# Reordering the expert stage of a pre-norm attention and mixture-of-experts block: the next expert's rows and weights prepared under this one's products, the down product by halves of its contraction, and its last 64-row chunk as two column halves

## The chip, the cores and the metric

The kernel runs on one core of one Trainium2 chip. The metric is the device time of one launch in microseconds; the median of three launches is given, and beside it one execution under the hardware profiler.

## What is computed

The reference is one transformer layer over 16 sequences of 512 tokens, 512 features wide. The first half is layer norm, attention with 16 heads of 32, an output projection and a residual sum. The second half is layer norm, a router, 32 routed experts and one shared expert, and a residual sum. What the change touches is the part for the routed experts:

```python
C = int(math.ceil(CF * T / E))                 # 8192 tokens, 32 experts: 320 slots for each expert
...
Xp = x[slots_token].reshape(E, C, d)           # gather of rows, d = 512
G = jnp.einsum('ecd,edi->eci', Xp, W_gate)     # 512 -> 256
U = jnp.einsum('ecd,edi->eci', Xp, W_up)       # 512 -> 256
Y = jnp.einsum('eci,eid->ecd', jax.nn.silu(G) * U, W_down)   # 256 -> 512
Yf = Y.reshape(EC, d) * slots_w[:, None]
out = jnp.zeros((T, d), x.dtype).at[slots_token].add(Yf)
```

## The kernel before, in words

`transformer_block` runs three parts one after the other: `setup`, `sequences` (attention, router and shared expert for 16 sequences, with 8192 by 4 scatters of routing records into a table in DRAM), and `experts`. Only `experts` is changed. It has one program for each engine, tied together by semaphores; nothing is planned at run time, and the order on each engine is the order written.

Every matrix product is made of three float16 products (`product`, L194 to L198): each operand is scaled and split into a high and a low half, and high by high, high by low and low by high are summed in PSUM. The splitting of an operand takes two instructions: ScalarE writes the high half (`ACT.Copy` with a scale), and VectorE writes what is left (`scalar_tensor_tensor`: input times scale minus high half).

The 320 rows of an expert are taken as three chunks (`CS` = 3) of 128, 128 and 64 rows (`LASTC` = 64). `q` is the parity of the expert, for buffers that exist twice: the raw weights, the split weights, the gathered rows `xg`, the result `y`. For expert e:

* SyncE loads the three raw weights of expert e + 2 (`load`, L1142) as soon as VectorE has split those of expert e.
* GpSimd, in this order: indirect gathers of the rows of expert e + 2 into `xg` (`gather`, L1162, three DMAs), a copy of the slots' indices (L1180), a wait for the three finished chunks of `y` of expert e and for the scatters of expert e - 1, and three indirect DMAs that add `y` to the output in DRAM (L1190).
* TensorE: 48 matmuls for gate and up (L1226; two blocks `j` of 128 hidden features, each gate, then up, each 4 parts of the contraction times 3 float16 products, 320 columns); then the transposes of the first two chunks of rows of expert e + 1 (L1213, float32, 4 for a chunk); then the down product chunk by chunk (L1241; for each chunk, both halves `j` of the contraction, 3 matmuls of 512 columns each), with the transposes of the third chunk ahead of the third chunk's down product. The third chunk's matmuls have 64 weight columns (shape 128*64).
* ScalarE: tanh of the two gate blocks (L1272), the high halves of the hidden activations (L1275), the high halves of two chunks of transposed rows (L1262), the scaled results of the down product (L1286), and last, for expert e + 2, the high halves of the three weights (L1255).
* VectorE: the gating multiplications (L1328, L1331) of both blocks, the low halves of the hidden activations (L1334), the low halves of the transposed rows (L1316), and last the low halves of the three weights of expert e + 2 (L1308).

The transposed and split rows `xT` exist once, so the splitting of expert e + 1's rows follows the last gate and up product of expert e. The transposes go in turn to two PSUM banks (`dense2` and `o_ps`), the down results in turn to two others.

## Time and profile before

| what | us |
|---|---|
| median of 3 launches (2461.67 to 2462.29) | 2461.91 |
| the profiled execution | 2484.26 |
| its span | 2482.3 |
| setup and sequences, in the span | to about 2055 |
| experts, in the span | about 2055 to 2482 |

The profiled execution is 22.35 us longer than the median launch, and 1.96 us of it lie outside its span. Times below are positions in that span. Busy time of an engine is the union of its instructions. A matmul's duration counts from its issue to its modelled end, so successive matmuls overlap: what sets the pace is the distance from one start to the next.

### The profile page before, as it was taken

Reading aid. Unit: us, or ns where it says so; the run is one execution under the profiler, and the core shown is the slowest. Engines: PE = TensorE matmul, PEld = TensorE weight load, DVE = VectorE, ACT = ScalarE, POOL = GpSimd, SP = SyncE. Lnnn points to the kernel's source line nnn. Section 1 sums busy time; section 2 is a strip of 40 time slices with the busy share of each in tenths; the row PEclk is TensorE's granted clock in tenths of the full one; section 3 lists DMA queues with packets and bytes.
Section 4 is the critical chain, followed back from the end, with each engine's and each line's share of the span. In section 5 each row is a group of like instructions: output and inputs, shape, how many; then the busy total and the mean of one; then the engine's idle time right before and its main releaser. Section 6 shows DMA issues by size and latency. Waiting matters only on the chain. (4 is left out here: it accounts for less than half of the span.)

```text
span 2482.3 us, 48737 instructions
## 1 busy us (share of the span) xinstructions
PE 2293.4 (92%) x15466; PEld 1152.8 (46%) x15466; DVE 1584.5 (64%) x4870; ACT 1079.3 (43%) x1849; POOL 1125.8 (45%) x1622
## 2 busy tenths in 40 slices
PE   3789999999999999999999999999997786999997
PEld 1334444444444444444444444444443334666664
DVE  4355667666767676767676766666757554666664
ACT  3344444444443434444444444444432214666664
POOL 2234143444444444444344444445333534777775
PEclk8889999999999999999999999999999997999999
DMA  4212222222222222222222212121212017888886
GB/s 168 69 45 64 56 71 62 65 62 64 70 62 68 65 61 61 62 61 61 61 62 61 78 44 78 44 77 48 73 31 74 27 40 201 238 234 236 235 234 116
DMA packets 180850, 222.52 MB, mean 90 GB/s; under 512 B 37776, under 2 KB 119792, under 8 KB 180624
## 3 DMA queue, kind: packets, MB, share of 16 engines
q1 hardware_dynamic: 154000, 177.58, 24.3%
q0 software_dynamic: 26624, 42.12, 7.6%
q8 instruction: 118, 1.93, 0.4%
q14 instruction: 108, 0.88, 0.1%
HBM read 112.65 MB, written 56.46 MB: 68 GB/s over the span
## 5 line engine op out<-in xcount | busy, mean ns | idle before, releaser
L942 DVE CUSTOM_DVE_ANT_0 junk<-scores,maskrow 128x512 f16<-128x512 f32 (+3 forms) x1024 | 465.0, 486 | 186.0 <-PE scores L548 123.3
L674 ACT ACTIVATE probs<-scores_T 128x512 f32<-128x512 f32 x640 | 371.8, 597 | 206.4 <-PE scores_T L563 196.8
L1062 POOL TENSOR_SCALAR_AFFINE_SELECT probs<-probs 128x256 f32<-128x256 f32 x512 | 192.2, 414 | 305.2 <-ACT probs L674 303.9
L1071 POOL DMA_INDIRECT slots_dram<-rec,idx x256 | 257.4, 1006 | 119.1 <-issue 76.9
L548 PE MATMUL scores<-stack_k,stack_q 96*128 96x512 f16 (+3 forms) x1024 | 249.6, 305 | 57.9 <-DVE nmax L942 56.4
L563 PE MATMUL scores_T<-stack_q,stack_k 97*128 97x512 f16 (+3 forms) x1024 | 246.6, 302 | 21.3 <-ACT probs L674 9.8
L1048 POOL TENSOR_TENSOR xres<-xres,bo 128x512 f32<-128x512 f32 x64 | 81.2, 1271 | 265.3 <-DMA xres<-in_x 265.3
L196 PE MATMUL dense<-xT_hi,wqkv_hi 128*128 128x512 f16 x512 | 196.8, 384 | 1.5 <-DVE xT_lo L913 1.5
L197 PE MATMUL dense<-xT_lo,wqkv_hi 128*128 128x512 f16 x512 | 195.5, 382 | 0.0
L198 PE MATMUL dense<-xT_hi,wqkv_lo 128*128 128x512 f16 x512 | 195.5, 382 | 0.0
L1190 POOL DMA_INDIRECT out<-ex_y,ex_sidx x96 | 151.6, 1579 | 76.5 <-issue 41.0
L548 PEld LDWEIGHTS scores<-stack_k,stack_q 96*128 96x128 f16 x1024 | 96.1, 99 | 191.2 <-DVE nmax L942 102.6
L631 ACT ACTIVATE glu<-dense,bqk 128x512 f32<-128x512 f32 x128 | 88.0, 687 | 214.1 <-PE dense L198 207.4
L1054 POOL TENSOR_TENSOR split_q<-glu,split_q 128x512 f16<-128x512 f32 x64 | 74.3, 1161 | 215.0 <-ACT split_q L631 214.9
L563 PEld LDWEIGHTS scores_T<-stack_q,stack_k 97*128 97x128 f16 x1024 | 98.2, 98 | 137.9 <-ACT probs L674 15.7
L572 PE MATMUL o_ps<-probs,v 128*32 128x512 f32 (+3 forms) x2048 | 153.2, 440 | 7.8 <-POOL probs L1062 6.6
L572 PE MATMUL scores_T<-probs,ones 128*32 128x256 f32 (+3 forms) x2048 | 155.4, 436 | 3.6 <-issue 3.1
L913 DVE SCALAR_TENSOR_TENSOR xT_lo<-dense,xT_hi 128x512 f16<-128x512 f32 x128 | 86.7, 689 | 94.6 <-ACT xT_hi L622 85.7
L1168 POOL DMA_INDIRECT ex_xg<-x2n_dram,ex_gidx x96 | 120.2, 1252 | 47.1 <-POOL ex_gidx L1163 27.6
L956 DVE STREAM_TRANSPOSE denT<-scores_T 128x512 f32<-128x512 f32 x64 | 45.7, 714 | 143.7 <-PE scores_T L572 135.8
L1030 POOL TENSOR_SCALAR mv<-mv 128x1 f32<-128x1 f32 x128 | 35.6, 278 | 215.6 <-DVE mv L723 209.5
L646 ACT ACTIVATE glu<-dense 128x512 f32<-128x512 f32 x64 | 38.2, 597 | 209.9 <-PE dense L198 133.4
(229 smaller groups left out, 5520.0 us busy)
## 6 DMA issues: line engine op xcount, KB each, us to landing
stack_q<-split_q SPq DMA_DIRECT2D x384, 64.0 KB
stack_k<-split_k SPq DMA_DIRECT2D x384, 64.0 KB
out<-xres SPq DMA_DIRECT2D x67, 256.0 KB, 3.0
xres<-in_x SPq DMA_DIRECT2D x64, 256.0 KB, 2.8
x2n_dram<-x2n SPq DMA_DIRECT2D x16, 1024.0 KB, 4.3
ex_raw_wg<-in_W_gate SPq DMA_DIRECT2D x32, 512.0 KB
ex_raw_wu<-in_W_up SPq DMA_DIRECT2D x32, 512.0 KB
ex_raw_wd<-in_W_down SPq DMA_DIRECT2D x32, 512.0 KB
```

Of the source, the lines that this page charges most:

```text
L196: pe.matmul(out, w[0], x[0], start=start, stop=False)
L197: pe.matmul(out, w[0], x[1], start=False, stop=False)
L198: return pe.matmul(out, w[1], x[0], start=False, stop=stop)
L548: last = pe.matmul(bank[:, at:at + cols], c["stack_q"][0:SROWS, hg, h, qt * P:(qt + 1) * P], c["stack_k"][0:SROWS, hg, h, 0:cols], start=T ...
L563: last = pe.matmul(bank[:, at:at + cols], c["stack_k"][0:SROWS + 1, hg, h, kt * P:(kt + 1) * P], c["stack_q"][0:SROWS + 1, hg, h, kt * P:k ...
L572: last = pe.matmul(bank[h * HD:(h + 1) * HD, kt * P:SEQ], loaded(kt, h), c["probs"][:, h, PCOL[kt]:PCOL[kt] + n], start=kt == 0, stop=kt = ...
L674: act.activation(to, at, ACT.Exp, scale=SCALE / (QS * QS)).then_inc(exp_done, 1)
L942: last = dve.tensor_tensor_reduce(out=c["junk"][:, f % 2, at:at + cols], in0=ps["scores"][f % 2][:, at:at + cols], in1=c["maskrow"][:, SEQ ...
L1062: last = pool.affine_select(out=blk, in_=blk, compare_op=ALU.is_ge, fill=0.0, base=0, pattern=[[0, 2], [1, P]], channel_multiplier=-1)
L1071: pool.indirect_dma_start(out=a["slots"], out_offset=bass.IndirectOffsetOnAxis(ap=c["idx"][:, t, k:k + 1], axis=0), in_=c["rec"][:, t, k, ...
L1168: pool.indirect_dma_start(out=e_["xg"][q][0:r, ch, :], out_offset=None, in_=a["x2n"], in_offset=bass.IndirectOffsetOnAxis(ap=e_["gidx"][q] ...
L1190: pool.indirect_dma_start(out=a["out"], out_offset=bass.IndirectOffsetOnAxis(ap=e_["sidx"][q][0:r, ch:ch + 1], axis=0), in_=e_["y"][q][0:r ...
```

## The change

In words:

* `xT` exists twice, by parity, and the three chunks of transposes have three banks (`dense2`, `scores1`, `scores0`); the three chunks of down results have three others (`dense0`, `dense1`, `o_ps`).
* TensorE makes the transposes of the next expert's first chunk between the two blocks `j` of gate and up, and those of the second and third chunk after the second block. The down product of the two 128-row chunks is done for the first half `j` of the contraction and then for the second, with a wait for the hidden activations ahead of each half. The 64-row chunk then takes 12 matmuls of 256 columns in place of 6 of 512: the left half of the columns goes to PSUM partitions 0 to 63 and the right half to partitions 64 to 127.
* ScalarE and VectorE split the weights of expert e + 1 (not e + 2) during expert e: gate ahead of the first tanh, up after it, down later. On VectorE the low half of the down weights is the last item of the expert. The hidden activations of the first block are split before the second block is gated.
* The result of the 64-row chunk is evicted as 128 partitions by 256, and scattered as 128 half rows of 1 KB in place of 64 rows of 2 KB. For that a second table of indices (`at`) and of weights is made once, ahead of the first expert.
* SyncE's program is unchanged; the semaphore that it waits for (`w_ready`) now moves at another time.

The core of the diff:

```diff
+        out_halves = a["out"].rearrange("t (h d) -> (t h) d", h=2)
...
-            pool.wait_ge(table_ready, 2)
+            pool.wait_ge(table_ready, 1)
...
             gather(1, 1)
+            pool.wait_ge(table_ready, 5)
...
-                pool.tensor_copy(e_["sidx"][q][:, :], e_["tok"][:, bass.ds(e * CS, CS)]).then_inc(sidx_ready, 1)
+                pool.tensor_copy(e_["sidx"][q][:, :], e_["at"][:, bass.ds(e * CS, CS)]).then_inc(sidx_ready, 1)
...
                 for ch in range(CS):
-                    r = rows(ch)
+                    to, of = (a["out"], e_["y"][q][:, ch, :]) if ch < CS - 1 else (out_halves, e_["y"][q][:, ch, 0:D // 2])
...
+            T_BANK = (ps["dense"][2], ps["scores"][1], ps["scores"][0])
+            Y_BANK = (ps["dense"][0], ps["dense"][1], ps["o"])
...
             def expert(e, q, more):
-                pe.wait_ge(w_ready, (e + 1) * 3)
                 pe.wait_ge(xT_copied, (e + 1) * CS)
...
                 for j in range(JB):
                     for n, w in enumerate(("wg", "wu")):
+                        if j == 0:
+                            pe.wait_ge(w_ready, e * 3 + n + 1)
                         for k in range(DK):
...
-
+                    if j == 0 and more:
+                        transposes(e + 1, 1 - q, 0)
                 if more:
-                    transposes(e + 1, 1 - q, range(CS - 1))
-                for ch in range(CS):
-                    if ch == CS - 1 and more:
-                        transposes(e + 1, 1 - q, [ch])
...
+
+                    pe.wait_ge(glu_ready, e * 2 * JB + 2)
+                    transposes(e + 1, 1 - q, 1)
+                    transposes(e + 1, 1 - q, 2)
+                pe.wait_ge(w_ready, (e + 1) * 3)
+                for j in range(JB):
+                    pe.wait_ge(h_ready, e * JB + j + 1)
+                    for ch in range(CS - 1):
+                        if j == 0 and not is_first(e, 1):
+                            pe.wait_ge(y_ready, (e - 1) * CS + ch + 1)
+                        last = product(pe, Y_BANK[ch][:, :], both(e_["hT"], ALL, j, slice(ch * P, (ch + 1) * P)), both(e_["wd"][q], ALL, j, ALL),
+                                       j == 0, j == JB - 1)
+                        if j == JB - 1:
+                            last.then_inc(y_done, 1)
+                if not is_first(e, 1):
+                    pe.wait_ge(y_ready, e * CS)
+                for j in range(JB):
+                    h, w = both(e_["hT"], ALL, j, slice((CS - 1) * P, CAP)), both(e_["wd"][q], ALL, j, ALL)
+                    for n, (hh, ww) in enumerate(((h[0], w[0]), (h[0], w[1]), (h[1], w[0]))):
+                        for half in range(2):
+                            last = pe.matmul(Y_BANK[CS - 1][half * LASTC:(half + 1) * LASTC, 0:D // 2], hh, ww[:, half * (D // 2):(half + 1) * (D // 2)],
+                                             start=j == 0 and n == 0, stop=j == JB - 1 and n == 2)
+                last.then_inc(y_done, 1)
...
             def expert(e, q, more):
-                for j in range(JB):
...
                 if more:
-                    copies(e + 1, 1 - q, range(CS - 1))
+                    weights_hi(e + 1, 1 - q, 0)
+                tanh(e, 0)
+                if more:
+                    weights_hi(e + 1, 1 - q, 1)
+                    copies(e + 1, 1 - q, 0)
+                hidden(e, 0)
+                tanh(e, 1)
+                if more:
+                    weights_hi(e + 1, 1 - q, 2)
+                hidden(e, 1)
+                if more:
+                    copies(e + 1, 1 - q, 1)
+                    copies(e + 1, 1 - q, 2)
                 if not is_first(e, 2):
                     act.wait_ge(y_added, (e - 1) * CS * 16)
                 act.wait_ge(wcol_ready, e + 1)
                 for ch in range(CS):
...
+                    act.wait_ge(y_done, e * CS + ch + 1)
+                    cols = D if rows(ch) == P else D // 2
+                    act.activation(e_["y"][q][:, ch, 0:cols], Y_BANK[ch][:, 0:cols], ACT.Copy, scale=e_["wcol"][q][:, ch:ch + 1]).then_inc(y_ready, 1)
...
+            dve.tensor_scalar(e_["twice"][:, 0, 0:LASTC], pairs_v[:, 0:LASTC, 0], 2.0, None, ALU.mult).then_inc(table_split, 1)
+            dve.tensor_scalar(e_["twice"][:, 0, LASTC:P], pairs_v[:, 0:LASTC, 0], 2.0, 1.0, ALU.mult, ALU.add).then_inc(table_split, 1)
+            dve.tensor_copy(e_["twice"][:, 1, 0:LASTC], pairs_v[:, 0:LASTC, 1]).then_inc(table_split, 1)
+            dve.tensor_copy(e_["twice"][:, 1, LASTC:P], pairs_v[:, 0:LASTC, 1]).then_inc(table_split, 1)
...
             def expert(e, q, more):
                 dve.tensor_copy(e_["wcol"][q][:, :], e_["w"][:, bass.ds(e * CS, CS)]).then_inc(wcol_ready, 1)
...
                 if more:
-                    copies(e + 1, 1 - q)
-                if more == 2:
-                    weights_lo(e + 2, q)
+                    weights_lo(e + 1, 1 - q, 0)
+                gated(e, 0)
+                if more:
+                    weights_lo(e + 1, 1 - q, 1)
+                    copies(e + 1, 1 - q, 0)
+                hidden(e, 0)
+                gated(e, 1)
+                hidden(e, 1)
+                if more:
+                    copies(e + 1, 1 - q, 1)
+                    copies(e + 1, 1 - q, 2)
+                    weights_lo(e + 1, 1 - q, 2)
...
-                  "xT": [sb2(f"ex_xT_{h}", [P, DK, CAP], F16) for h in ("hi", "lo")],
+                  "twice": sb2("twice", [nr, 2, P]), "tok": sb2("slot_tok", [P, nr], I32), "at": sb2("slot_at", [P, nr], I32), "w": sb2("slot_w", [P, nr]),
+                  "xT": [[sb2(f"ex_xT{q}_{h}", [P, DK, CAP], F16) for h in ("hi", "lo")] for q in range(2)],
```

On ScalarE the high half of the gate weights now waits for the raw weights of expert e + 1 and for the last gate and up product of expert e - 1; it stands in the queue ahead of `tanh(e, 0)`.

## Rows read from the trace of the kernel before

**Rows 1.** The page: span, and busy time of each engine.
```profile
span 2482.3 us, 48737 instructions
PE 2293.4 (92%) x15466; PEld 1152.8 (46%) x15466; DVE 1584.5 (64%) x4870; ACT 1079.3 (43%) x1849; POOL 1125.8 (45%) x1622
```

**Rows 2.** Busy time in stretches: PE, PEld, DVE, ACT, POOL, clock, DMA share, GB/s.
```profile
2130.36:2425.60 295.24, 289.48 (x1874) 180.29 (x1873) 191.40 (x313) 188.26 (x313) 218.15 (x193) 1.00 0.84 234
2254.00:2263.00 9.00, 8.75 (x55) 4.92 (x54) 4.88 (x8) 6.84 (x11) 7.15 (x7) 1.00 1.05 295
2263.60:2266.60 3.00, 3.00 (x25) 2.30 (x23) 2.80 (x7) 1.02 (x3) 1.85 (x2) 1.00 0.33 62
```

**Rows 3.** Timeline of one expert on PE and DVE: start, duration, idle before.
```profile
2253.36 0.60 PE L1213 MATMUL o_ps<-ident,ex_xg 128*128 128x128 f32 x4
2253.65 0.49 DVE L1331 TENSOR_TENSOR ex_glu<-ex_glu,scores_T 128x320 f32<-128x320 f32 x1 [0.17 <-PE scores_T L198]
...
2254.06 1.11 DVE L1334 SCALAR_TENSOR_TENSOR ex_hT_lo<-ex_glu,ex_hT_hi 128x320 f16<-128x320 f32 x2
...
2254.65 0.39 PE L196 MATMUL dense<-ex_wd_hi,ex_hT_hi 128*128 128x512 f16 x1 [0.25 <-DVE ex_hT_lo L1334]
...
2257.34 0.46 PE L1213 MATMUL o_ps<-ident,ex_xg 64*128 64x64 f32 x4
...
2257.73 0.40 PE L196 MATMUL dense<-ex_wd_hi,ex_hT_hi 128*64 128x512 f16 x1
...
2258.83 0.38 PE L198 MATMUL dense<-ex_wd_hi,ex_hT_lo 128*64 128x512 f16 x1
2259.14 0.31 PE L196 MATMUL scores<-ex_xT_hi,ex_wg_hi 128*128 128x320 f16 x1
...
2265.68 0.60 PE L1213 MATMUL dense<-ident,ex_xg 128*128 128x128 f32 x4
```

**Rows 4.** Waits of PE from 2130 to 2425 us: total, times, longest.
```profile
PE dense L196 <- DVE ex_hT_lo L1334: 5.8, 24, 0.3
```

**Rows 5.** Timeline of PE and its weight loads: attention's 32-column matmuls, and a 64-column load.
```profile
1708.42 2.36 PE L572 MATMUL o_ps<-probs,v 128*32 128x512 f32 x32
...
1709.30 0.13 PEld L572 LDWEIGHTS o_ps<-probs,v 128*32 128x32 f32 x4 [0.30 <-issue]
...
1710.71 0.39 PE L196 MATMUL dense<-xT_hi,sgT_hi 128*128 128x512 f16 x1
...
2442.35 0.11 PEld L197 LDWEIGHTS dense<-ex_wd_lo,ex_hT_hi 128*64 128x64 f16 x1
```

**Rows 6.** Timeline of POOL's indirect DMAs, with VectorE's weight splitting beside one.
```profile
2111.47 0.90 POOL L1168 DMA_INDIRECT ex_xg<-x2n_dram,ex_gidx  x1 [0.30 <-issue]
...
2114.47 1.22 DVE L1308 SCALAR_TENSOR_TENSOR ex_wu_lo<-ex_raw_wu,ex_wu_hi 128x1024 f16<-128x1024 f32 x1
2114.63 2.57 POOL L1190 DMA_INDIRECT out<-ex_y,ex_sidx  x1 [2.06 <-DMA out<-ex_y,ex_sidx]
...
2252.12 1.64 POOL L1190 DMA_INDIRECT out<-ex_y,ex_sidx  x1 [1.12 <-issue]
2254.07 1.58 POOL L1190 DMA_INDIRECT out<-ex_y,ex_sidx  x1 [0.30 <-PE o_ps L1213]
2255.96 1.45 POOL L1190 DMA_INDIRECT out<-ex_y,ex_sidx  x1 [0.30 <-issue]
...
2258.47 1.03 POOL L1168 DMA_INDIRECT ex_xg<-x2n_dram,ex_gidx  x1 [0.86 <-POOL ex_gidx L1163]
...
2261.09 1.83 POOL L1168 DMA_INDIRECT ex_xg<-x2n_dram,ex_gidx  x1 [0.30 <-issue]
...
2264.44 1.63 POOL L1190 DMA_INDIRECT out<-ex_y,ex_sidx  x1 [1.12 <-issue]
```

**Rows 7.** Timeline of SyncE's queue: the first of three weight loads of an expert.
```profile
2252.34 0.37 SPq L1144 DMA_DIRECT2D ex_raw_wg<-in_W_gate  x1
```

**Rows 8.** Timeline of PE: first down matmul of the last expert.
```profile
2463.89 0.38 PE L196 MATMUL dense<-ex_wd_hi,ex_hT_hi 128*128 128x512 f16 x1 [1.07 <-DVE ex_hT_lo L1334]
```

More of the change, by code:

```diff
@@ L1202, in _, with transposes @@
                 pe.transpose(ps["scores"][w][:, 0:nr], e_["split"][:, w, :], e_["ident"][0:nr, 0:nr]).then_inc(table_T, 1)
-            def transposes(e, q, chunks):
-                pe.wait_ge(gathered[q], arrived(e, q, CS))
-                for ch in chunks:
-                    r, m = rows(ch), e * CS + ch
-                    if not (isinstance(e, int) and m < 2):
-                        pe.wait_ge(xT_copied, m - 1)
-                    settle(pe)
-                    bank = [ps["dense"][2], ps["o"]][(q * CS + ch) % 2]
-                    for k in range(DK):
-                        last = pe.transpose(bank[:, k * P:k * P + r], e_["xg"][q][0:r, ch, k * P:(k + 1) * P], e_["ident"][0:r, 0:r])
-                    last.then_inc(xT_done, 1)
-            transposes(0, 0, range(CS))
+            for w in range(2):
+                pe.transpose(ps["scores"][2 + w][:, 0:nr], e_["twice"][:, w, :], e_["ident"][0:nr, 0:nr]).then_inc(table_T, 1)
+            T_BANK = (ps["dense"][2], ps["scores"][1], ps["scores"][0])
+            Y_BANK = (ps["dense"][0], ps["dense"][1], ps["o"])
+            def transposes(e, q, ch):
+                r = rows(ch)
+                if ch == 0:
+                    pe.wait_ge(gathered[q], arrived(e, q, CS))
+                settle(pe)
+                for k in range(DK):
+                    last = pe.transpose(T_BANK[ch][:, k * P:k * P + r], e_["xg"][q][0:r, ch, k * P:(k + 1) * P], e_["ident"][0:r, 0:r])
+                last.then_inc(xT_done, 1)
+            pe.wait_ge(table_ready, 5)
+            for ch in range(CS):
+                transposes(0, 0, ch)
             def expert(e, q, more):
-                pe.wait_ge(w_ready, (e + 1) * 3)
                 pe.wait_ge(xT_copied, (e + 1) * CS)
@@ L1265, in _ @@
[L1265 to L1277 removed]
+            T_BANK = (ps["dense"][2], ps["scores"][1], ps["scores"][0])
@@ new lines, in copies, with tanh @@
+            def copies(e, q, ch):
+                r = rows(ch)
+                act.wait_ge(xT_done, e * CS + ch + 1)
+                act.activation(e_["xT"][q][0][:, :, ch * P:ch * P + r], T_BANK[ch][:, :].rearrange("p (k t) -> p k t", k=DK)[:, :, 0:r],
+                               ACT.Copy, scale=XS).then_inc(xT_hi, 1)
+            def tanh(e, j):
+                act.wait_ge(gu_done, e * 2 * JB + 2 * j + 1)
+                act.activation(e_["glu"][:, j, :], ps["scores"][2 * j][:, 0:CAP], ACT.Tanh, scale=0.5 / (XS * WS)).then_inc(tanh_ready, 1)
@@ new lines, in hidden @@
+            def hidden(e, j):
+                act.wait_ge(glu_ready, e * 2 * JB + 2 * j + 2)
+                act.activation(e_["hT"][0][:, j, :], e_["glu"][:, j, :], ACT.Copy, scale=HS / (XS * WS) ** 2).then_inc(h_hi, 1)
+            for n in range(3):
+                weights_hi(0, 0, n)
+            for ch in range(CS):
+                copies(0, 0, ch)
+            def expert(e, q, more):
+                if more:
+                    weights_hi(e + 1, 1 - q, 0)
[11 more added lines that the diff above has]
+                    copies(e + 1, 1 - q, 2)
@@ L1319, in _ @@
-            weights_lo(0, 0)
-            copies(0, 0)
-            weights_lo(1, 1)
+            dve.wait_ge(table_T, 4)
+            dve.wait_ge(table_ready, 3)
+            last = slice(CS - 1, E * CS, CS)
+            dve.tensor_copy(e_["at"][:, last], ps["scores"][2][:, last]).then_inc(table_ready, 1)
+            dve.tensor_copy(e_["w"][:, last], ps["scores"][3][:, last]).then_inc(table_ready, 1)
+            dve.wait_ge(table_ready, 5)
+            T_BANK = (ps["dense"][2], ps["scores"][1], ps["scores"][0])
@@ L1323, in expert @@
+            for n in range(3):
+                weights_lo(0, 0, n)
+            for ch in range(CS):
+                copies(0, 0, ch)
             def expert(e, q, more):
                 dve.tensor_copy(e_["wcol"][q][:, :], e_["w"][:, bass.ds(e * CS, CS)]).then_inc(wcol_ready, 1)
[L1325 to L1331 removed]
```

102 lines of the change are left out of this document (36 added, 66 removed).

## The prediction

> **What bounds the kernel now.** The page comes first: over the whole span TensorE is busy 92% of the time and no other engine above 64% [rows 1]. The change touches only the last 430 us, so the next view is the busy time of the steady experts, 24 of them in 295.24 us: 12.30 us for an expert, TensorE busy 98%, its clock at 2.4 GHz throughout, VectorE 191.40/24 = 7.97 us, ScalarE 7.84 us, GpSimd 9.09 us, and the DMA engines at 84% [rows 2]. TensorE sets the pace, and the others are close enough to matter once it is faster.
>
> The timeline shows what an expert is made of on TensorE [rows 3]. From the first product (2259.14) to the next transposes (2265.68) the 48 gate and up matmuls take 6.54, 0.136 each. Two chunks of transposes take 0.44 each (2253.36 to 2254.24). Then nothing starts until 2254.65, 0.41 later: VectorE gates the second block only after its last product (2253.65, 0.49 long) and then splits the first. The row puts 0.25 of this down as a wait; it occurs in all 24 experts, 5.8 us in total [rows 4]. From 2254.65 two chunks of down product run, 12 matmuls at 0.2165 (2.60), to 2257.25. There is a gap of 0.09 to the third chunk's transposes (2257.34), 0.39 for them, 1.32 for its six matmuls (2257.73 to 2259.05) and 0.09 to the next expert. The sum is 6.54 + 0.88 + 0.41 + 2.60 + 0.09 + 0.39 + 1.32 + 0.09 = 12.32 against the 12.30 of the long stretch. The 0.09 stands wherever the shape of the array's use changes.
>
> GpSimd is the second reading. Its rows show no wait for data, yet its cycle is exactly the same (2252.12 to 2264.44) [rows 6]. It is held by VectorE. A gather of the third chunk takes 0.90 when nothing is in its way (2111.47) and 1.83 in the steady state (2261.09). A first scatter takes 1.64, but 2.57 when it starts at 2114.63 under a weight split (2114.47, 1.22 long): it is held until that instruction ends. So a GpSimd instruction that starts during a weight split waits for its end. Without this its cycle would be three scatters with their gaps (2252.12 to 2257.41) 5.29, to the first gather 1.06, to the third 2.62, the third 0.90, and about 1.1 for the copy and the issue of the next scatter: 10.97. So 12.32 - 10.97 = 1.35 us an expert are now spent held, at no cost.
>
> **The change, part by part, for one expert.**
>
> *Wait for the hidden activations.* New order on TensorE, from the first product at 0: block 0 to 3.27, transposes of chunk 0 to 3.71, block 1 to 6.98, transposes of chunks 1 and 2 with one switch to 7.90, down for half 0 to 9.20, for half 1 to 10.50. The first half's activations come from block 0. VectorE does ahead of them: gate split, gating of block 0, up split, a copy. Up's last product of block 0 ends at 3.4; then 0.49 + 1.22 + 0.7 + 0.5 gives about 6.3, and 7.90 is when they are needed. The second half: last product 7.1, gating to 7.6, high half on ScalarE (about 0.5) to 8.1, low half to 8.7; needed at 9.20. The 0.41 goes away. If VectorE were more than 0.5 late it would come back, as a wait ahead of half 1. **-0.41.**
>
> *Transposes.* As many as before, 1.27 us. Those of chunk 0 now stand between two products of 128*128; from products to transposes there was no gap today (2265.54 + 0.136 = 2265.68), and the way back isn't seen clean. Between 0 and 0.09; I take 0.05. **+0.05.** They need the gathered rows at 3.3 instead of 6.5. The third gather of the steady state ends its issue at 2262.92 and its rows are used at 2265.68, so landing takes at most 2.76.
>
> *The 64-row chunk.* Now 6 matmuls at 0.22: 1.32. After: 6 pairs of 256 columns on the two halves of the array's columns. If a pair runs together it takes 256 columns' time, 0.107 (half of 0.2165 and a bit less). Attention's products are the same kind with four groups of 32 columns [rows 5]: 32 instructions from 1708.42 to 1710.71, 2.29 us. They have 2 passes x 4 groups x (512 + 384 + 256 + 128) columns = 10240 columns, which one after another at 0.2165 for 512 would be 4.33 us even at one cycle a column. Four weight loads share 0.13 us. So groups do overlap. A float32 transpose of 128 columns takes 0.11 here [rows 3], two cycles a column; 8 steps (4 sizes, 2 passes) at that pace with the groups fully overlapped are 2.13 us, so each step costs 0.02 more. That gives 6 x (0.107 + 0.02) = 0.76, plus one more switch of 0.09. Bounds: 0.64 with perfect overlap and no extra switch, 1.41 with none. A single 64-column weight load takes 0.11 [rows 5], as long as the pair's product, so it hides only while it runs beside it; I stay with 0.76 + 0.09. **-0.47.**
>
> The Trainium skill (TensorE: Matmul & The Clock Gate, Part 3, "The mechanism") says that weight loads overlap running matmuls only when the row group differs. These pairs share their rows, and by it a pair would be load plus product; that is the second rival below. No row here separates this for a pair of 64.
>
> *ScalarE and VectorE* do the same work in another order; the last eviction has 256 elements a partition instead of 512 (about -0.2 us, hidden). 7.97 and 7.84 of 11.5 leave room. *Weights:* SyncE's load is released by the last split, now at the end of the expert before (about -0.3), and its data is wanted by ScalarE at about 0.8 of the next expert: about 12.5 us after issue. Today an expert's load is issued at 2252.34 [rows 7], the DMA engines are full from 2254 to 2263 and down to a third from 2263.6 [rows 2], so it lands within 11.5 us together with scatters and gathers. Hidden by 1 us. *Scatter:* 64 more descriptors; on GpSimd the third takes 1.58 like the second rather than 1.45, +0.13. The same bytes move; at worst every half row costs what a row did. DMA work per expert, 0.84 x 12.30 = 10.3 us, becomes 90% of 11.5.
>
> *Sum:* 12.30 - 0.41 + 0.05 - 0.47 = 11.47, a gain of 0.83, over the 31 distances between starts of experts: -25.7.
>
> *Ends.* In front of the first expert VectorE makes four more small copies (+0.5), and three banks for the transposes free the first products of a wait (-0.5): zero. After the last product the down product now waits 1.07 [rows 8] for both blocks; half 0 will run in that time: -1.07; the chunk's halves -0.47 more, the last eviction -0.2, the third scatter +0.13, and half 1 may still wait 0.4. About -1.2.
>
> Total -26.9. The sum is against the profiled execution, 2484.26 - 26.9 = 2457.4. It is 22.35 above the median of the runs; nothing says that this excess lies in the experts, so I carry the difference over whole: 2461.91 - 26.9 = **2435.0**.
>
> **Rivals.**
>
> *GpSimd becomes the bound (ends slower).* Its unheld cycle becomes 10.97 + 0.13 = 11.10. Today three splits stand back to back and hold it for 1.35 in all. After, they stand apart, near 1.9, 4.0 and 9.8, and each can hold an instruction up to 1.2, in all 3.6. Gathers are then late, and the transposes inside the products wait. Held more than 0.37 an expert, GpSimd decides; more than 1.2, the kernel is slower than before. Eight instruction starts, each with chance 3.66/11.5 to meet a split and 0.6 to wait, would be 1.5: 12.6 us an expert, +0.3 x 31 = +9, 2470. Against it: the first scatter waits for the last eviction of y, so GpSimd's cycle is tied at about 1.7 in each expert. Following its durations from there the other two scatters start near 3.6 and 5.5, the gathers near 8.3, 9.6 and 10.9: each just beside a split, held about 0.2 in all. The margins are some 0.2 us, so 9% for slower, and 5% for a mild form (11.9 us, 2448).
>
> The Trainium skill (SBUF — State Buffer, "SBUF: two separate sides") has this as an exclusive lock on a port pair, for VectorE instructions with two SBUF inputs; the rows for the weight splits agree. By it the two splits of hidden activations hold GpSimd too, up to 0.5 each.
>
> *Pairs do not overlap.* The 64-row chunk takes 1.32 + 0.09 as 12 matmuls. Expert 12.30 - 0.41 + 0.05 + 0.09 = 12.03, -8.4 - 0.7: 2452.8. For it: the 0.11 of a load. Against it: attention's rows. 12%.
>
> *Weights late.* The full DMA stretch grows with a shorter expert; ScalarE's split stands ahead of tanh, so a late load stops all. 0.5 us late an expert: 12.0, 2451. 6%.
>
> *No change that can be measured*, as the product of mild forms of these: 2%.
>
> **Numbers.** The forecast has 66%, for 2428 to 2441: an expert of 11.25 (perfect pairs, no switches) to 11.65 (second half waits 0.2). Range 2427 to 2454: it reaches over the pairs that don't overlap and late weights; outside are the slow case, no change and a little at the fast side. A change of 0.2%, 4.9 us, is about what a measurement can tell from none. Faster: 66 + 12 + 6 + 5 less 1 = 88%; same 3%; slower 9%.
>
> **What would show it.** Distance between the first transposes of two experts 11.5 (12.0: no overlap). The two matmuls of a pair starting within 0.02 us, six pairs in 0.76. No wait of the first down matmul for the low half of the hidden activations. GpSimd's third gather near 0.9 to 1.1, and its first scatter waiting for ScalarE's y. The transposes of chunk 0 without a wait for a DMA: if they do wait, GpSimd or the DMA queues bound the stage, and the prediction is wrong. ScalarE's gate split waiting for the raw weights would show the other failure.

## The result and the profile after

The changed kernel takes 2523.4 us (median of 4 runs, 2518.5 to 2527.7) against 2462.1 for the kernel before on the same chip: 1.0246 times as long, with a 95% interval of 1.022 to 1.0272. It is slower by 61 us where 27 us faster were forecast.

The profiled execution took 2519.45 us, its span 2517.5. The part ahead of the experts differs by up to 32 us among the profiled executions of this document, so from here on the measure is the *stage*: from the load of the slot table to the end of the span. It is read from one profiled execution of each kernel, so it comes without an interval; the ratios have one. It was 2054.97 to 2482.3 = 427.3 before, and is 2030.34 to 2517.5 = 487.2 after, 59.9 more. That is the whole loss, within 1.4 us.

The busy times after, in the same form as [rows 2] (columns: window, its length, busy time with number of instructions on each engine, TensorE's clock as a share of 2.4 GHz, share of the DMA engines' time, GB/s). The first row is 300 us of steady experts; the last two are the stall and what follows it in the expert shown below:

```profile
core 0: us, PE busy (x) PEld busy (x) DVE busy (x) ACT busy (x) POOL busy (x), PEclk, DMA share, GB/s
2100.00:2400.00 300.00, 251.88 (x1685) 161.73 (x1682) 160.85 (x264) 154.78 (x261) 198.78 (x162) 0.90 0.81 197
2239.00:2240.00 1.00, 1.00 (x11) 0.81 (x8) 0.49 (x1) 0.14 (x2) 0.91 (x1) 1.00 1.00 107
2248.00:2250.00 2.00, 0.00 (x0) 0.00 (x0) 0.70 (x1) 0.00 (x0) 2.00 (x1) 1.00 1.08 358
2250.30:2257.20 6.90, 5.89 (x23) 3.64 (x24) 1.58 (x3) 2.34 (x4) 5.22 (x5) 0.51 0.86 120
```

TensorE, at 98% before, is busy for 252 of 300 us and its mean clock is 0.90. The DMA engines' share did not rise (0.81), but an expert takes longer: at the mean distance of 14.37 us given below it is 11.6 us of DMA time for each, against 0.84 x 12.30 = 10.3 before, for the same bytes (222.52 MB in the whole kernel, before and after). What TensorE waits for, over all experts (total us, times, longest):

```profile
PE dense L1219 <- DMA ex_xg<-x2n_dram,ex_gidx: 60.5, 15, 5.1
```

Before, the steady experts had no wait for gathered rows. The timeline of two experts on TensorE shows its place (start, duration, and in brackets the idle time ahead and what ended it):

```profile
2242.74 0.30 PE L1261 MATMUL o_ps<-ex_wd_hi,ex_hT_hi 128*64 128x256 f16 x2
2242.87 0.28 PE L1261 MATMUL o_ps<-ex_wd_lo,ex_hT_hi 128*64 128x256 f16 x2
...
2243.31 0.28 PE L1261 MATMUL o_ps<-ex_wd_hi,ex_hT_lo 128*64 128x256 f16 x2
2243.52 0.31 PE L196 MATMUL scores<-ex_xT_hi,ex_wg_hi 128*128 128x320 f16 x1
...
2246.65 0.30 PE L198 MATMUL scores<-ex_xT_hi,ex_wu_lo 128*128 128x320 f16 x1
2251.31 1.08 PE L1219 MATMUL dense<-ident,ex_xg 128*128 128x128 f32 x4 [4.36 <-DMA ex_xg<-x2n_dram,ex_gidx]
2252.20 0.47 PE L196 MATMUL scores_T<-ex_xT_hi,ex_wg_hi 128*128 128x320 f16 x1
2252.46 0.47 PE L197 MATMUL scores_T<-ex_xT_lo,ex_wg_hi 128*128 128x320 f16 x1
...
2257.39 0.30 PE L198 MATMUL scores_T<-ex_xT_hi,ex_wu_lo 128*128 128x320 f16 x1
...
2262.33 0.31 PE L196 MATMUL scores<-ex_xT_hi,ex_wg_hi 128*128 128x320 f16 x1
```

The reader is to see three things. First, the expert without a stall is as designed: its first product is at 2232.16 and the next expert's at 2243.52, 11.36 us later, and of the six pairs of its 64-row chunk the first starts at 2242.74, the second at 2242.87 and the last at 2243.31. Second, in the next expert the transposes of chunk 0, now between the two blocks, start at 2251.31 after 4.36 us without work, on the landing of a gather. Third, what follows runs at half speed until about 2257.3: the four transposes take 1.08 instead of 0.60, the products stand 0.27 apart instead of 0.136. The last window above, which begins 1.0 us ahead of the end of the wait, has a clock of 0.51, the 1.2 GHz level; earlier in the wait (2248 to 2250) it was 1.00. Each of the 13 long waits (4.0 to 5.1 us) is followed by 3 us with a clock of 0.50 to 0.54. From 2243.52 to 2262.33 the expert takes 18.81: 11.36, 4.52 more from the product of 2246.65 to the transposes than the 0.136 of a product, and 2.93 left for the low clock.

Read for all experts, the distance between first products is 11.36 for every second one and 17.0 to 19.5 (mean of 13: 18.1) for those between. 13 times 6.74 is 87.6 us, close to the 86.8 from the forecast for the stage (427.3 - 26.9 = 400.4) to the 487.2 measured.

GpSimd and SyncE ahead of that stall (same columns; the first row is the VectorE split that the first scatter meets):

```profile
2233.72 1.23 DVE L1357 SCALAR_TENSOR_TENSOR ex_wg_lo<-ex_raw_wg,ex_wg_hi 128x1024 f16<-128x1024 f32 x1 [1.92 <-ACT ex_wg_hi L1283]
2233.76 2.67 POOL L1193 DMA_INDIRECT out<-ex_y,ex_sidx  x1 [4.64 <-issue]
2236.74 2.05 POOL L1193 DMA_INDIRECT out<-ex_y,ex_sidx  x1 [0.30 <-issue]
...
2240.08 0.88 POOL L1165 COPY ex_gidx<-slot_tok 128x3 int32 x1
...
2244.62 0.91 POOL L1170 DMA_INDIRECT ex_xg<-x2n_dram,ex_gidx  x1 [0.30 <-issue]
2245.53 0.95 POOL L1183 COPY ex_sidx<-slot_at 128x3 int32 x1
2247.60 2.60 POOL L1193 DMA_INDIRECT out<-ex_y,ex_sidx  x1 [1.12 <-issue]
```

```profile
2243.31 0.37 SPq L1146 DMA_DIRECT2D ex_raw_wg<-in_W_gate  x1
```

The third gather is issued from 2244.62 to 2245.53, and the three weight loads, 1.5 MB, are issued from 2243.31 on. The chain of work that ended last has issue and landing of the gather as one piece of 6.56 us, so it lands at 2251.18, 5.65 us after the end of its issue:

```profile
2244.62 6.56 DMA ex_xg<-x2n_dram,ex_gidx
```

The landing of the gathers over 300 us (each of the three counted from the start of its own issue: shortest, median, longest) is

```profile
DMA to landing us min/median/max: 2.9/3.5/7.5
```

For the third gather alone, the one issued at 2244.62 and then the one issued at 2257.66, it is

```profile
DMA to landing us min/median/max: 6.6/6.6/6.6
...
DMA to landing us min/median/max: 3.1/3.1/3.1
```

These two stand for all 20 experts between 2100 and 2400. In ten of them the weight load is issued some 2 us ahead of the end of the third gather's issue; that gather lands 5.5 to 6.6 us after that end, and TensorE stalls. In the other ten the load is issued later, 1.6 us or more behind that end, and the gather lands in 2.0 to 2.5 us.

### The profile page after: what moved, and what is told of

It is laid out like the page before. It is cut to its first block and busy times, and to the rows that moved or that the text cites. A ratio compares the mean times of both kernels' runs of the same rounds, so it can differ in the third digit from the quotient of the medians.

```text
span 2517.5 us, 49134 instructions
## 1 busy us (share of the span) xinstructions
PE 2293.5 (91%) x15660; PEld 1165.2 (46%) x15660; DVE 1584.7 (63%) x4877; ACT 1074.2 (43%) x1849; POOL 1142.2 (45%) x1622
## 2 busy tenths in 40 slices
DMA packets 182899, 222.52 MB, mean 88 GB/s; under 512 B 37777, under 2 KB 123889, under 8 KB 182673
## 5 line engine op out<-in xcount | busy, mean ns | idle before, releaser
L1193 POOL DMA_INDIRECT out<-ex_y,ex_sidx x96 | 185.9, 1936 | 117.2 <-issue 96.3
L572 PE MATMUL scores_T<-probs,ones 128*32 128x512 f32 (+3 forms) x2048 | 151.1, 436 | 0.0
L622 ACT ACTIVATE xT_hi<-dense 128x512 f16<-128x512 f32 x128 | 72.9, 600 | 107.3 <-PE dense L505 102.0
```

The lines of the kernel that those rows point to most:

```text
L572: last = pe.matmul(bank[h * HD:(h + 1) * HD, kt * P:SEQ], loaded(kt, h), c["probs"][:, h, PCOL[kt]:PCOL[kt] + n], start=kt == 0, stop=kt = ...
L1193: pool.indirect_dma_start(out=to, out_offset=bass.IndirectOffsetOnAxis(ap=e_["sidx"][q][:, ch:ch + 1], axis=0), in_=of, in_offset=None, co ...
```

## The experiments

All stand on the changed kernel or the one before, and every ratio is to the kernel before in the same session. "Distance" is the mean between first gate products of successive experts; "waits" are those for gathered rows on TensorE between 2100 and 2400, with their number. Stage, distance, waits, clock and DMA share are of one profiled execution each. The sessions ran on different chips, so where an expectation names a time, the ratio times 2462.1 is what to hold against it.

| kernel | ratio, 95% | stage us | distance us | waits us (n) | mean clock | DMA share |
|---|---|---|---|---|---|---|
| before | 1 | 427.3 | 12.37 | 0 | 1.00 | 0.84 |
| the change | 1.0246 (1.022 to 1.0272) | 487.2 | 14.37 | 44.7 (10) | 0.90 | 0.81 |
| gather_first | 0.9969 (0.9947 to 0.9991) | 422.5 | 12.07 | 13.6 (9) | 0.99 | 0.90 |
| whole_chunk | 1.0272 (1.0232 to 1.0311) | 498.2 | 14.71 | 33.2 (12) | 0.93 | 0.79 |
| eighth_loads | 1.0026 (1.0007 to 1.0046) | 433.0 | 12.62 | 25.6 (16) | 0.99 | 0.67 |
| halves_only | 1.0012 (0.9997 to 1.0027) | 430.0 | 12.48 | 2.9 (1) | 0.99 | 0.85 |
| back | 1.0037 (1.0023 to 1.005) | 429.3 | 12.51 | 18.9 (20) | 0.99 | 0.90 |
| gf_back | 1.0014 (1.0001 to 1.0026) | 428.7 | 12.23 | 17.3 (18) | 0.99 | 0.90 |
| small_split | 1.0185 (1.0166 to 1.0205) | 471.6 | 13.86 | 37.0 (11) | 0.92 | 0.80 |
| gf_eighth | 0.9923 (0.9903 to 0.9943) | 404.1 | 11.49 | 1.1 (2) | 1.00 | 0.69 |
| load_after | 1.0002 (0.9993 to 1.0012) | 426.8 | 12.43 | 18.1 (20) | 0.99 | 0.85 |
| spread | 1.0066 (1.0049 to 1.0082) | 440.8 | 12.87 | 32.1 (22) | 0.99 | 0.86 |
| gf_spread | 0.9947 (0.993 to 0.9963) | 412.7 | 11.71 | 6.8 (6) | 1.00 | 0.96 |
| gf_rows_spread | 0.9937 (0.9917 to 0.9957) | 414.7 | 11.84 | 10.9 (7) | 1.00 | 0.95 |

### One part of the change alone: halves_only

The kernel before with nothing but the column halves of the 64-row chunk and their scatter as half rows:

```diff
-                        last = product(pe, ps["dense"][(q * CS + ch) % 2][0:r, :], both(e_["hT"], ALL, j, slice(ch * P, ch * P + r)),
...
+                        for n, (hh, ww) in enumerate(((h[0], w[0]), (h[0], w[1]), (h[1], w[0]))):
+                            for half in range(2):
+                                last = pe.matmul(bank[half * LASTC:(half + 1) * LASTC, 0:D // 2], hh, ww[:, half * (D // 2):(half + 1) * (D // 2)],
...
```

> The kernel before with only the 64-row chunk changed to two column halves, with its half-row scatter. The pairs save 0.57 us an expert on TensorE if nothing else binds: 2462 - 18 = about 2444 us. Theory A: the gathers are used 3 us later in the expert than in the changed kernel, so most of the gain comes through: 2444 to 2456 us. Theory B: the extra DMA time of the half rows makes gathers late here too: 2465 us or more.

No change: 1.0012, or 2465 us. Neither theory: the rows wait only once between 2100 and 2400 (2.9 us, in the one expert that takes 17.9). The timeline of an undisturbed expert shows both the gain and where it went (PE is TensorE, ACT ScalarE, DVE VectorE):

```profile
2280.35 0.46 PE L1218 MATMUL o_ps<-ident,ex_xg 64*128 64x64 f32 x4
...
2280.74 0.30 PE L1256 MATMUL dense<-ex_wd_hi,ex_hT_hi 128*64 128x256 f16 x2
...
2281.04 0.38 ACT L1277 ACTIVATE ex_xT_hi<-o_ps 128x256 f16<-128x256 f32 x1
...
2281.31 0.28 PE L1256 MATMUL dense<-ex_wd_hi,ex_hT_lo 128*64 128x256 f16 x2
2281.45 0.42 DVE L1343 SCALAR_TENSOR_TENSOR ex_xT_lo<-o_ps,ex_xT_hi 128x256 f16<-128x256 f32 x1 [1.95 <-ACT ex_xT_hi L1277]
...
2282.15 0.31 PE L196 MATMUL scores<-ex_xT_hi,ex_wg_hi 128*128 128x320 f16 x1 [0.57 <-issue]
```

Six pairs run from 2280.74 to 2281.42, 0.68 instead of 1.32. But the third chunk's rows, transposed at 2280.35, are split on ScalarE until 2281.42 and on VectorE until 2281.87, and the next expert's first product needs them: it starts at 2282.15 after 0.57 of idle time. From the third chunk's transposes to that product it is 1.80 us, exactly as before (2257.34 to 2259.14 in [rows 3]); before, the longer chunk filled this time. GpSimd's cycle is the same as well, 2286.60 to 2298.86. So the distance stays 12.23 (before 12.31) in the undisturbed experts. The pairs give their 0.6 in the change, where the transposes stand ahead; which of the two paths, the splits or GpSimd's cycle, would hold them back alone was not tried.

### Half rows or order: whole_chunk

The change with the 64-row chunk as before: 6 matmuls of 512 columns, one scatter of 64 whole rows.

```diff
-                    to, of = (a["out"], e_["y"][q][:, ch, :]) if ch < CS - 1 else (out_halves, e_["y"][q][:, ch, 0:D // 2])
+                    r = rows(ch)
...
+                        out=a["out"], out_offset=bass.IndirectOffsetOnAxis(ap=e_["sidx"][q][0:r, ch:ch + 1], axis=0),
```

> The 64-row chunk is put back: 6 matmuls of 512 columns, 64 rows of 2 KB scattered; all else as in the changed kernel. Theory A: the late gathers stay, the undisturbed expert is 0.56 us longer, so the wait is a little shorter: 2500 to 2530 us. Theory B: the scatters' DMA time falls by about 1.7 us an expert, the gathers land in time, and the time is 2450 us or less.

Slower still, 1.0272 (2529 us, at the upper end of Theory A), with an undisturbed distance of 12.00 and the stalled ones at 17.3 to 19.1. So half rows are not what makes the gathers late; the rest of the change does it without them.

### The queue on GpSimd: gather_first

The gathers of expert e + 2 are issued ahead of the scatters of expert e - 1 instead of behind them:

```diff
             def expert(e, q, more):
                 if more == 2:
                     pool.wait_ge(xT_done, (e + 1) * CS)
                     gather(e + 2, q)
-                ...                                    # the scatters of expert e stood here
+                if not (isinstance(e, int) and e == 0):
+                    scatter(e - 1, 1 - q)
```

> GpSimd issues the gathers of expert e + 2 ahead of the scatters of expert e - 1, not behind them. Theory A (the gathers are issued too late, because they stand behind scatters that wait for y, and then need about 6 us to land beside the weight load): they are issued some 5 us earlier, the wait of the transposes for them goes away, the clock stays up, and an expert takes the 11.35 us that the undisturbed ones show: about 2434 us. Theory B (the DMA engines are the limit, with the half rows' extra work): the wait moves elsewhere and the time stays above 2480 us. Theory C (VectorE's weight splits hold GpSimd too often, wherever its instructions stand): GpSimd's cycle of 11.1 plus holds of 1 us or more bounds an expert: 2450 to 2490 us.

The stage falls from 487.2 to 422.5, so when the gathers are issued is enough to undo the loss. Theory A has the cause, but not its time: by the ratio it is 2454 us, not 2434. Against the forecast's 400.4, 22 us are missing. GpSimd shows the new wait:

```profile
2267.72 1.55 POOL L1189 DMA_INDIRECT out<-ex_y,ex_sidx  x1 [0.30 <-issue]
...
2276.58 1.63 POOL L1189 DMA_INDIRECT out<-ex_y,ex_sidx  x1 [1.48 <-DMA out<-ex_y,ex_sidx]
```

The third scatter is issued by 2269.27, and the first of the next expert starts at 2276.58 once it has landed. That is 7.3 us, beside a weight load that is issued up to 2269.15.

### The transfers beside it: eighth_loads and small_split

eighth_loads is the change with 16 of the 128 partitions of each weight loaded from the third expert on; small_split the change with VectorE's low halves of the weights made for 64 elements a partition in the steady experts (of 1024; the expectation's 2048 is a slip). Both leave out work.

```diff
-                    load(e + 2, q)
+                    for name, of in WEIGHTS:
+                        sp.dma_start(e_["raw_" + name][q][0:16, :, :], ...[e + 2, 0:16])
```

```diff
-                dve.scalar_tensor_tensor(e_[name][q][1][:, :, :], e_["raw_" + name][q][:, :, :], WS, ...)
+                k, n_ = (slice(None), slice(None)) if isinstance(e, int) else (slice(0, 1), slice(0, 64))
+                dve.scalar_tensor_tensor(e_[name][q][1][:, k, n_], e_["raw_" + name][q][:, k, n_], WS, ...)
```

> From the third expert on only 16 of 128 partitions of each weight are loaded (an eighth of the bytes; the rest of the weights keeps old values). Theory A: the gathers are still issued about 1.4 us ahead of their use in every second expert, but land in under 3 us instead of 6; the wait falls from 4.4 to at most 1.5 us and the clock stays up: 2435 to 2455 us. If landing is not slowed by the weight load, the time stays near 2520 us. Theory C, holds alone: no change, near 2520 us.

> The changed kernel, but in the steady experts VectorE's split of each weight covers 64 of each partition's 2048 elements (the low halves are then not the reference's). It measures what the 1.22 us weight splits cost by holding GpSimd and by their own time. Theory H (the holds are a large part of the late gathers): first scatters 1.63 instead of 2.6 to 2.7, gathers 0.9 to 1.1, GpSimd 2 to 3 us an expert earlier, waits for rows fall from 60 us to under 20, stage from 487 to under 450. Theory O (order and landing beside the weight load alone): the scatters and gathers get shorter, but the weight load is released earlier too and the gathers still land beside it: waits 40 us or more, stage above 465.

Less load traffic takes away 54 of the 60 us (433.0), the holds only 16 (471.6). Neither comes out as expected in every number: eighth_loads is at 2468 us, not 2435 to 2455, with waits up to 2.3 us, and small_split fits Theory O (stage above 465, and 45.9 us of waits over the whole stage, where the change has 60.5). In small_split the scatters aren't held. Behind a stall GpSimd even sits idle for 5.94 us, because TensorE has not yet come to the end of y:

```profile
2285.35 1.68 POOL L1193 DMA_INDIRECT out<-ex_y,ex_sidx  x1 [5.94 <-issue]
```

From one first scatter to the next it takes 11.4 there where TensorE doesn't stall, so GpSimd keeps pace, and yet every second expert has its stall. One of them, GpSimd first and then TensorE:

```profile
2267.05 0.91 POOL L1170 DMA_INDIRECT ex_xg<-x2n_dram,ex_gidx  x1 [0.30 <-issue]
...
2267.66 0.31 PE L196 MATMUL scores<-ex_xT_hi,ex_wg_hi 128*128 128x320 f16 x1
...
2273.95 0.73 PE L1219 MATMUL dense<-ident,ex_xg 128*128 128x128 f32 x4 [2.85 <-DMA ex_xg<-x2n_dram,ex_gidx]
```

The issue of the third gather ends at 2267.96, only 0.3 us behind the expert's first product and 3.0 us ahead of the need at 2270.9. The rows are there 6.0 us after that end, beside a weight load issued from 2266.45 on. In the change the same issue ended 2.0 us behind the first product (2245.53 and 2243.52). VectorE's holds are real, 1.0 us for the first scatter and 0.5 for the second in the rows of the change above, and with them the gathers come 1.7 us later, but they are a minor part.

### When rows are needed: back and gf_back

The transposes of chunk 0 stand behind block 1 again; gf_back has the gathers first as well.

```diff
-                    if j == 0 and more:
-                        transposes(e + 1, 1 - q, 0)
                 if more:
+                    transposes(e + 1, 1 - q, 0)
                     pe.wait_ge(glu_ready, e * 2 * JB + 2)
```

The splits of chunk 0 move as well, behind those of the hidden activations.

> The changed kernel, but the transposes of the next expert's chunk 0 stand behind the products of block 1 again, with those of chunks 1 and 2 (and their copies behind both halves of the hidden activations); GpSimd's order is as in the change. Theory N (the rows are needed too early: 3.3 us after the expert's start where they were needed at 6.5): the waits for gathered rows on TensorE, 60.5 us in 15 experts, shrink by up to 3.3 us each and with them the half-speed clock behind them; expert pair from 29.4 to about 24, time below 2460. Theory Q (one ring through GpSimd's queue, the weight load and the landing of rows sets the pace, wherever the rows are used): waits of about 1 us an expert stay, pair 26 to 28, time 2475 to 2510. If the early use had no part at all: 2523 as in the change.

> As the one with the transposes of chunk 0 behind block 1, and GpSimd also issues the gathers of an expert ahead of the scatters of the one before. Theory N: both halves of the cause gone, no wait for rows left on TensorE, its own 11.4 to 11.6 us an expert: experts' stage about 402 us, 27 less than before, ratio about 0.99. Theory Q (scatter, its landing and the next scatter are one chain): GpSimd's waits for landed scatters, 9.5 us in 300 in the one with gathers first, stay or grow, 12.3 to 12.8 us an expert, ratio 0.995 to 1.005.

back comes to 429.3, 58 us less than the change. Its waits are shorter but more of them:

```profile
PE dense L1219 <- DMA ex_xg<-x2n_dram,ex_gidx: 18.9, 20, 1.9
```

20 waits of at most 1.9 us, and the mean clock stays at 0.99. With 2471.3 us and 25.0 for a pair of experts it lies between its two theories. With both edits (428.7) nothing more is gained: its distances are 11.36 for eight experts near the start and mostly 12 to 13 behind. The stage of 402 expected by Theory N of gf_back does not come; its ratio, 1.0014, is in Theory Q's range. The late scatter landings of Theory Q are there too, but it is ScalarE that waits for them and not GpSimd:

```profile
ACT ex_y L1328 <- DMA out<-ex_y,ex_sidx: 38.8, 17, 3.9
```

### When the load runs: load_after and spread

load_after holds the weight load until the next expert's rows have landed; spread issues each of the three loads as soon as its own buffer is free.

```diff
                     sp.wait_ge(w_ready, (e + 1) * 3)
...
+                    sp.wait_ge(gathered[1 - q], arrived(e + 1, 1 - q, CS))
...
                     load(e + 2, q)
```

```diff
-                    sp.wait_ge(w_ready, (e + 1) * 3)
...
-                    load(e + 2, q)
+                    for n, (name, of) in enumerate(WEIGHTS):
+                        sp.wait_ge(w_ready, e * 3 + n + 1)
...
+                        sp.dma_start(e_["raw_" + name][q][:, :, :], ...[e + 2])
```

> The changed kernel, but SyncE issues a weight load only once the rows of the next expert have landed (in the trace of the change the load of 2243.31 runs over the third gather, issued by 2245.53 and landed at 2251.2). Theory L (the weight load stretches the landing to 5 or 6 us): the gathers land within 3 us of their issue, the waits for rows on TensorE fall from 44.7 us in 300 to under 20; in their place the weights come up to 3 us later, and if they come after 0.8 us of the next expert ScalarE's gate split waits for them. Stage 440 to 465 against 487. If the landing is slow for another reason (the software queue's own backlog of scatters ahead of the gathers): waits for rows stay above 40 us, weights are late on top, stage 490 or more.

> The changed kernel, but each of the three weight loads is issued as soon as its own buffer's split is done (one early in an expert, one in the middle, one at its end) and not all three at the last. The same bytes, 4 to 9 us earlier and in three portions, so at most a third of them runs over the gathers. Theory L: stage 430 to 450 (with an eighth of the bytes it was 433.0). Theory B (the total of DMA work bounds it): stage 480 to 490, DMA share as before the edit.

load_after takes the whole loss away (426.8, ratio 1.0002), more than Theory L hoped for, although it only ever delays a transfer. Its waits between 2100 and 2400:

```profile
POOL out L1195 <- DMA out<-ex_y,ex_sidx: 24.5, 17, 2.2
...
ACT ex_wg_hi L1285 <- DMA ex_raw_wd<-in_W_down: 23.2, 16, 2.0
...
PE dense L1221 <- DMA ex_xg<-x2n_dram,ex_gidx: 18.1, 20, 2.5
```

The rows still cost 18.1 us, and 23.2 us have moved to ScalarE, which now waits for late weights, 24.5 to GpSimd, which waits for landed scatters. The landing of the gathers in it:

```profile
DMA to landing us min/median/max: 3.1/4.6/5.9
```

The longest is 5.9 instead of 7.5, while the median is higher, and not within 3 us as Theory L had it: what went away are the worst landings. They were those of the third gather, the one that TensorE waits for: from the end of its issue it now lands in 2.0 to 3.4 us in all 24 experts, where it took 5.5 to 6.6 in every second one. The first two gathers are the slower ones now. spread comes to 440.8, 46 less than the change, as its Theory L expected.

### Together: gf_eighth, gf_spread, gf_rows_spread

> Gathers issued ahead of the scatters, and from the third expert on only 16 of the 128 partitions of each weight loaded (output not the reference's). If the weight load's share of the DMA engines is what is left in the one with gathers first (stage 422.5): TensorE alone sets the pace, 11.4 us an expert, stage 398 to 405, GpSimd's first scatter no longer waiting for a landed scatter. If GpSimd's own cycle (two copies, six DMA issues, held by splits) is what is left: 12.3 to 12.8 us an expert stays, stage 418 to 424.

```profile
2100.00:2400.00 300.00, 298.90 (x2210) 198.75 (x2209) 207.78 (x344) 202.38 (x342) 215.34 (x206) 1.00 0.69 129
```

With gathers first and an eighth of the load bytes (row as in the windows above) TensorE is busy 298.9 of 300 us, and 27 of the distances are 11.36: nothing else stands in the way, and the stage is as expected for the first case.

> Gathers issued ahead of the scatters and the weight loads in three portions. With gathers first the stage was 422.5 and with an eighth of the bytes 404.1, so 18 us hang on the weight loads. Theory L (when they run): most of these come back, stage 404 to 412, faster than before by 0.6 to 0.9%. Theory B (how much there is to move: 0.90 of the DMA engines' time already): 418 to 424, ratio 0.995 to 0.999.

> As the one with gathers first and loads in three portions, but ScalarE evicts the second column half of the 64-row chunk to partitions 0 to 63 in an instruction of its own, and the scatter moves 64 whole rows again instead of 128 half rows. GpSimd's third scatter 1.43 instead of 1.55, 64 fewer descriptors; ScalarE about 0.2 us more. If half rows cost DMA time: 1 to 4 us of the stage better than its neighbour. If not: within 1 us of it.

gf_spread does all the work and is faster than both kernels, 0.9947 with an interval clear of 1. Its stage of 412.7 is just above Theory L's range. Its first and last 100 us between 2100 and 2400:

```profile
2100.00:2200.00 100.00, 100.00 (x740) 66.31 (x739) 68.83 (x116) 68.22 (x115) 71.95 (x71) 1.00 0.99 254
...
2300.00:2400.00 100.00, 93.08 (x680) 60.58 (x679) 63.00 (x104) 60.81 (x105) 72.48 (x64) 1.00 0.93 221
```

For 22 experts it holds 11.36 with the DMA engines at 0.99 of their time (0.98 between 2200 and 2300); then six stand 12.4 to 13.0 apart. What it waits for between 2100 and 2400:

```profile
ACT ex_y L1331 <- DMA out<-ex_y,ex_sidx: 21.7, 8, 3.5
...
PE dense L1225 <- DMA ex_xg<-x2n_dram,ex_gidx: 6.8, 6, 1.4
```

Its neighbour with whole rows (ratio 0.9937, stage 2.0 us longer) can't be told from it. Half rows cost no DMA time that shows: an expert takes 0.96 x 11.71 = 11.2 us of it with them and 0.95 x 11.84 = 11.2 without. Both pay at the end: the scatters run an expert later, and from the last expert's first product to the end of the span it is 2442.8 - 2409.87 = 32.9 us, against 2482.3 - 2456.12 = 26.2 before (30.5 in the neighbour).

## Why the prediction was wrong

**Wait for the hidden activations (-0.41), transposes between products (+0.05), pairs (-0.47), sum 11.47: right.** Undisturbed experts are 11.36 apart, no wait for the low half of the hidden activations is left, and six pairs take 0.68 (forecast 0.76, and 0.09 for the switch behind them). The rival without overlap is refuted. The Trainium skill (TensorE: Matmul & The Clock Gate, Part 3, "The mechanism") says that a weight load overlaps running matmuls only when the row group differs. These pairs share their rows and start 0.11 apart, 256 columns' time, so for column halves the measurement decides against that sentence.

**The step that failed: "so landing takes at most 2.76", and with it that rows needed at 3.3 instead of 6.5 cost nothing.** As a reading of the kernel before the sentence was right, and it still holds in every second expert of the change (2.0 to 2.5); as a term of the changed kernel it was 5.5 to 6.6 in the others. 2.76 was read where no weight load runs: the one issued at 2252.34 [rows 7] has drained by 2263.6 [rows 2], and the next comes a period later, at about 2264.6, 1.7 us behind the end of the third gather's issue at 2262.92 [rows 6]. In the change the load is issued at 2243.31, 2.2 us ahead of that end (2245.53): the two have moved past each other by 3.9 us. The gather then shares the DMA engines with 1.5 MB and lands after 5.65.

By the prediction's own numbers the third gather ends near 11.8 (10.9 and 0.9) and the rows are needed at 11.47 + 3.3 = 14.8, which leaves 3.0 for the landing. small_split, without holds, has just this schedule, 3.0 left, and its rows come after 6.0. In the change the issue ends another 1.7 us later; so of the 4.4 us of the stall some 1.7 are late issue and the rest is the landing. The prediction moved the load ("about -0.3") and moved the need, and put neither beside the gather. The Trainium skill (DMA: Bandwidth & Descriptors, "Queues, rings and completion order") says that a DMA engine takes its queues in turn, a packet from each. That a gather beside a load lands late (7.5 us at the longest) agrees with it; no run here shows the turns themselves.

**GpSimd's cycle "tied at about 1.7", holds of 0.2: the second step.** The rival named the place and its consequence, at 9 and 5%. The gate split was put at 1.9 us behind the first product, just behind the first scatter's start; it starts at 1.56, 0.04 us ahead of the scatter (2233.72 and 2233.76, first product 2232.16), and the scatter takes 2.67. In the change GpSimd goes 13.84 us from one first scatter (2233.76) to the next (2247.60) where TensorE wants 11.36. Its unheld cycle was put at 11.10; in small_split it is 11.4, since the copy and the issue of the next scatter take 1.3 and not "about 1.1" (the 1.12 of idle time in [rows 6] leaves the copy nothing). What remains is about 1.0 on the first scatter, 0.5 on the second, about 0.9 on two copies (0.88 and 0.95 for 0.77 and 0.19) and 0.2 in a gap. These 2.5 us put GpSimd behind in each expert without a stall, and the stall lets it catch up. They are not why there is a stall in every second expert: small_split has the same period of two without them. There, behind a stall, the gathers have landed before TensorE's progress releases the next weight load, and in the expert after it the two meet again. The price of the rival was wrong too, since it counted no landing and no clock: 0.3 us an expert forecast, 2.0 measured.

**The low clock was in no term.** It costs 2.9 us in the expert shown, on top of 4.5 of waiting. In back, with 20 waits in 300 us and none above 1.9 us, the mean clock is 0.99; even there two of the waits, of 1.65 and 1.90 us, are followed by 3 us with a mean clock of 0.73 and 0.71, and another of 1.65 us is not.

**Which cause?** Late issue by GpSimd, the load beside the landing, and the early need act together, and none is the sole cause. Taking away any one gives back most: gathers first -65 us of the stage, the load held back -60, the need moved back -58, an eighth of the bytes -54, loads apart -46. The holds alone give back 16. Added up they are far more than the loss of 60, so they are not separate terms: each restores the same margin. This is argued from the figures; no run divides the loss among them.

**What bounds it next.** At 11.36 an expert TensorE is busy all the time (gf_eighth with the DMA engines at 0.69, the first 200 us of gf_spread with them at 0.98 to 0.99), so the DMA engines have next to nothing left. "DMA work becomes 90% of 11.5" was thus low by some 8 points, since DMA time per byte is no constant: the same bytes of an expert took 10.3 us of DMA time before, 11.2 in gf_spread (0.96 x 11.71) and 11.6 in the change, and in the change the engines moved 107 GB/s at a share of 1.00 in a scatter's window and 358 GB/s at 1.08 in a load's. Why gf_spread leaves the fast rhythm after 22 experts stays open; that more scatter landings are late there is in its waits, what sets it off isn't.

## What to carry to other kernels

Before moving a consumer forward, take the landing time of its transfer from the worst neighbour it can get after the change, and place every transfer that the change releases at another time on the same axis. When one engine gets faster, compare every other engine's cycle, holds included, with the new period: here a deficit of 2.5 us in 11.4 took 1.7 of the 3.0 us that the rows had for landing. A gain that stops at a neighbour's path, as that of the pairs did alone, can come through once the rest of the change has cleared that path.

## What the runs showed of the hardware that was not expected

* Two matmuls on the two column halves of the array, 64 columns each, with 256 moving columns: pairs 0.11 us apart, the time of one.
* In a wait of 4.36 us the granted clock fell to 1.2 GHz, and TensorE ran at it for the first 6 us behind the wait.
* A gather of 64 rows of 2 KB landed 2.0 to 2.5 us after the end of its issue where the load of 1.5 MB was issued behind it, and 5.5 to 6.6 us after it where the load was issued some 2 us ahead of that end.
* Delaying these 1.5 MB until the rows had landed shortened the stage by 60 us.
